# Choosing blocks of expert rows for half of the tokens, and normalising on ScalarE, in a kernel of two post-norm transformer layers

## The reference, cut to what matters

```python
# routing of layer 0; layer 1 is the same with softmax over all experts first, gelu, and hs + 0.3 * moe
logits = xf @ Wr + br                                   # 8 experts
topk_w, topk_idx = jax.lax.top_k(logits, 2)             # 2 chosen per token
gate = sum(one_hot(topk_idx, 8) * softmax(topk_w))
h = relu(einsum('th,ehf->etf', xf, W1) + b1)            # 128 -> 256, every expert
y = einsum('etf,efh->eth', h, W2) + b2                  # 256 -> 128
out = einsum('te,eth->th', gate, y)
layernorm: (x - mean) / sqrt(var + 1e-5)
```

## Time and profile before

| | us |
|---|---|
| median of 3 runs | 1236.21 (1231.8 to 1237.85) |
| the profiled execution's own time | 1233.06 |
| its span, first to last instruction | 1231.1 |
| TensorE busy | 1108.1 |
| VectorE busy | 883.3 |
| ScalarE busy | 753.3 |
| GpSimd busy | 274.9 |
| first expert stage, from its first up to the next attention's first scores | 307.6 to 440.7 |
| second expert stage, to the end | 1100.4 to 1231.1 |

### The profile page before, as it was taken

How to read it: one execution, slowest core, us unless ns; L and a number is a source line. 1 busy time by engine, 2 the same in 40 slices (tenths; PEclk the granted TensorE clock), 3 DMA queues, 4 the chain that set the end, 5 groups by cost and what they waited for, 6 DMA issues and landing times. The chain is left out here.

```text
span 1231.1 us, 24956 instructions
## 1 busy us (share of the span) xinstructions
PE 1108.1 (90%) x8797; PEld 606.1 (49%) x8872; DVE 883.3 (72%) x2136; ACT 753.3 (61%) x1505; POOL 274.9 (22%) x800
## 2 busy tenths in 40 slices
PE   5899998899999989999988998888888878899996
PEld 3466676656777745666555632212112212127775
DVE  3788767783445478888767888988999898914444
ACT  4377656567434426776656667677888767874332
POOL 8134322332002113433333310111101010100000
PEclk9899999999999999999999999999999999999998
DMA  3444343110001600344221311000211100000000
GB/s 87 122 112 110 93 96 89 47 36 8 1 1 27 157 20 31 81 100 101 66 74 31 64 35 30 22 11 15 40 35 34 29 11 17 7 1 1 10 9 18
DMA packets 40058, 57.70 MB, mean 47 GB/s; under 512 B 9495, under 2 KB 15079, under 8 KB 39679
## 3 DMA queue, kind: packets, MB, share of 16 engines
q1 hardware_dynamic: 39934, 56.11, 18.5%
HBM read 30.81 MB, written 24.64 MB: 45 GB/s over the span
## 5 line engine op out<-in xcount | busy, mean ns | idle before, releaser
L838 ACT ACTIVATE probs<-bank 128x512 f32<-128x512 f32 x1088 | 574.7, 603 | 268.9 <-PE bank L1206 267.4
L937 DVE TENSOR_REDUCE tile_max<-bank 128x1 f32<-128x512 f32 (+3 forms) x1152 | 612.0, 593 | 51.4 <-PE bank L1191 47.2
L1191 PE MATMUL bank<-qk 125*128 125x128 bf16 (+2 forms) x1664 | 389.2, 311 | 83.8 <-DVE tile_max L937 65.4
L1206 PE MATMUL bank<-qk 128*128 128x128 bf16 (+4 forms) x1608 | 362.6, 305 | 3.9 <-ACT probs L838 3.6
L1235 PE MATMUL bank<-probs,v_head 128*32 128x512 f32 (+3 forms) x3328 | 304.6, 455 | 0.1
L1191 PEld LDWEIGHTS bank<-qk 125*128 125x128 bf16 (+1 forms) x1664 | 133.6, 97 | 329.1 <-DVE tile_max L937 249.5
L1113 DVE SCALAR_TENSOR_TENSOR acc<-bank,gate,acc 128x128 f32<-128x128 f32 x256 | 72.0, 344 | 143.0 <-PE bank L1364 143.0
L1235 PEld LDWEIGHTS bank<-probs,v_head 128*32 128x32 f32 x3328 | 140.2, 109 | 50.2 <-issue 28.0
L1206 PEld LDWEIGHTS bank<-qk 128*128 128x128 bf16 (+1 forms) x1664 | 134.3, 96 | 52.7 <-ACT probs L838 16.8
L858 ACT ACTIVATE probs<-bank,sb_b 128x512 f32<-128x512 f32 x128 | 80.9, 683 | 123.3 <-PE bank L1353 123.3
L931 DVE TENSOR_REDUCE tile_max<-bank 128x4 f32<-128x512 f32 x128 | 87.4, 688 | 87.5 <-PE bank L1191 87.2
(11 more groups left out here) (130 smaller groups left out, 653.1 us busy)
## 6 DMA issues: line engine op xcount, KB each, us to landing
qk<-qk_parts SPq DMA_DIRECT2D x160, 144.0 KB
qk_parts<-q_parts SPq DMA_DIRECT2D x48, 192.0 KB, 2.4
qk_parts<-k_parts SPq DMA_DIRECT2D x48, 192.0 KB, 3.1
qk_parts<-q_parts SPq DMA_DIRECT2D x24, 96.0 KB, 2.3
qk_parts<-k_parts SPq DMA_DIRECT2D x24, 96.0 KB, 2.9
sb_w<-in_w SPq DMA_DIRECT2D x8, 256.0 KB, 3.8
sb_w<-in_w SPq DMA_DIRECT2D x2, 1024.0 KB, 5.3
qk<-neg_rows SPq DMA_DIRECT2D x96, 6.0 KB
```

The costliest lines, as they stand in the source:

```text
L838: nc.scalar.activation(probs[:, hd.probs_place(c), :], S2[i % len(S2)][:], ACT.Exp, scale=hd.a.scale).then_inc(sem("probs"), 1)
L937: ins = nc.vector.tensor_reduce(tile_max[:, hd.slot, t, which:which + 1], s1[:, at:at + P * count], AX.X, ALU.max)
L1191: ins = mm(s1[:, at:at + P * count], qk[hd.query_rows, hd.place, 0, P * t:P * (t + 1)], qk[hd.query_rows, hd.place, 1, P * k0:P * (k0 + co ...
L1206: ins = mm(s2[:, at:at + P * count], qk[hd.key_rows, hd.place, 1, P * j:P * (j + 1)], qk[hd.key_rows, hd.place, 0, P * q0:P * (q0 + count) ...
```

## The change

**Blocks for sequence 0.** The tokens of sequence 0 no longer go through all experts. Their 2048 pairs of token and chosen expert are laid into blocks of 128 rows of one expert each, `BLOCKS` = 23 (the most that can be needed), in `BLOCK_UNITS` = 6 units of up to 4 blocks. Sequence 1 stays dense: 16 units. So `UNITS` = 22. What this adds:

- Ahead of the stage, in the attention: `ranks` (nine small products that count, for each token and expert, the earlier tokens of that expert), `blocks` (which expert each block belongs to: `expert_i`), `slots` (the row of each pair: `places`), `biases` (`b1` by block), and 16 `scatter` steps, each an indirect DMA from GpSimd that writes 128 tokens' rows to their places in `x_blocks` in DRAM. That buffer is cleared by SyncE after heads 2 and 4 (1.5 MB each, one for each stage). In stage 1 the rows are first transposed back (`mtok`).
- Ahead of up(0), six places `IN_FRONT` without a unit, at which the attention's last steps and the first two `gx` stand. `gx` transposes a unit's rows (loaded from `x_blocks`) on TensorE, and VectorE copies them out.
- For each unit SyncE loads rows and the weights of each block, whose expert it reads from `expert_i` with `value_load`, into the SBUF space of the other stage's weights (two units' worth, used in turn). The load of w1 for unit m+2 waits for up(m), that of w2 for down(m).
- Each unit's result is copied by VectorE to `y_out`, stored by SyncE to `y_blocks`, and after the last one GpSimd gathers 16 x 128 rows by indirect DMA (`gather`, place 19); VectorE adds them with their weights (`combine`, places 26 and 31).
- The gate steps of sequence 0 move from the attention to places 13 to 21 of the stage.

**Normalising on ScalarE.** `normed` is gone. GpSimd computes besides `rstd` also `shift` = -mean * rstd (two more small instructions), and ScalarE does `x = rstd * x_plus + shift`, one instruction a tile. After an attention the two chunks of a sequence are normalised at two places instead of one.

The diff, cut to its core:

```diff
+TOP = 2
+BLOCKS = (TOP * S + E * (P - 1)) // P
+BLOCK_UNITS = -(-BLOCKS // TPC)
+UNITS = BLOCK_UNITS + CB * E
+IN_FRONT = 6
...
+first = at_unit(0, -1, 0)
+put_attention_out(0, 1, first, (0, 1, 2, 3, 4, 5, 6, 7, 9, 10))
+for m, i in enumerate((4, 5, 6, 8, 10, 12)):
+    put(later(first, i), ("gx", 0, m))
...
+            def load_w1(f, m):
+                for j in blocks_of(m):
+                    e = nc.sync.value_load(expert_i[0:1, j:j + 1], min_val=0, max_val=E - 1)
+                    sp.dma_start(block_weights(f)[0][:, TPC * (m % 2) + j % TPC, :],
+                                 inp[f"w1_{f}"][0][:, bass.ds(e, 1), :].rearrange("p a f -> p (a f)")
+                                 ).then_inc(sem(f"w1_in{m % 2}"), 16)
...
+            def first_blocks(f):
+                sp.wait_ge(sem("experts_known"), f + 1)
+                ge(sp, "y_ps", UNITS * f)
+                for m in range(2):
+                    load_w1(f, m)
+                for m in range(2):
+                    load_w2(f, m)
+                sp.wait_ge(sem("scattered"), 16 * TOP * TB * (f + 1))
+                for m in range(2):
+                    load_x(f, m)
+
+            def blocks(f):
+                for m in range(BLOCK_UNITS):
+                    n = len(blocks_of(m))
+                    if m + 2 < BLOCK_UNITS:
+                        taken(sp, "gx", f, m)
+                        load_x(f, m + 2)
+                        sp.wait_ge(sem("hid_ps"), UNITS * f + m + 1)
+                        load_w1(f, m + 2)
+                        sp.wait_ge(sem("y_ps"), UNITS * f + m + 1)
+                        load_w2(f, m + 2)
+                    sp.wait_ge(sem("y_taken"), UNITS * f + m + 1)
+                    sp.dma_start(y_blocks[f].rearrange("(j p) d -> p j d", p=P)[:, TPC * m:TPC * m + n, :],
+                                 y_out[:, m % 2, 0:P * n].rearrange("p (j d) -> p j d", d=D)
+                                 ).then_inc(sem(f"y_stored{m % 2}"), 16)
...
+            def gather(f, c):
+                for m in range(2):
+                    pool.wait_ge(sem(f"y_stored{m}"), 16 * BLOCK_UNITS // 2 * (f + 1))
+                for i in (0, 1):
+                    for t in range(TPC * c, TPC * (c + 1)):
+                        at = TB * i + t
+                        nc.gpsimd.indirect_dma_start(
+                            yg[:, at, :], None, y_blocks[f],
+                            bass.IndirectOffsetOnAxis(ap=places[:, at:at + 1], axis=0)).then_inc(sem(f"gathered{c}"), 16)
...
-            def normed(k, c):
-                dve.wait_ge(sem("rstd"), ROOT_OF[(k, c)])
-                for t in range(TPC * c, TPC * (c + 1)):
-                    ins = nc.vector.tensor_scalar(x[:, t, :], x_plus[:, t, :], mean_var[:, t, 0:1], rstd[:, t:t + 1],
-                                                  ALU.subtract, ALU.mult)
...
+                    if kind == "norm":
+                        k, c = which
+                        act.wait_ge(sem("rstd"), ROOT_OF[(k, c)])
+                        for t in range(TPC * c, TPC * (c + 1)):
+                            ins = nc.scalar.activation(x[:, t, :], x_plus[:, t, :], ACT.Identity,
+                                                       bias=shift[:, t:t + 1], scale=rstd[:, t:t + 1])
```

361 lines of the change are left out of this document (299 added, 62 removed).

## The result

The changed kernel takes **1286.64 us** (median of 4 runs, 1283.25 to 1288.13) against 1234.32 us for the one before in the same measurement: a ratio of 1.042, with a 95% interval of 1.038 to 1.045. It is 52 us slower. The forecast was slower too, but by 15 us: 1251 us. The result lies inside the range of 1220 to 1308.

A forecast was written before the change was run, and what follows sets the result against it. TensorE, busy 90%, was taken as the bound; removed units save 70 us, mostly eaten by SyncE's block loads. Terms 4.3 + 2.5 + 4 + 4 = +14.8 on 1233.1 give 1247.9, stated as 1251 us at the median; range 1220 to 1308.

The forecast's parts named there:

- the pace of the block units: Expert stages, between block units: SyncE's 8 weight loads, one load of rows and one store set a round, 11.7 us.
- rival A: Block rounds: issue is cheap, a load 0.7 us, a round 9.2 us, time 1222 us, faster; chance 0.28.
- The price of a load: SyncE's block weight loads: 0.59 issue, 0.05 gap and 0.65 for reading the expert's number, 1.3 us each.
- First stage: First expert stage: block rounds, dense units and 24 stores make the next attention start at 445.0 instead of 440.7, +4.3 us.
- Second stage: Second expert stage: block rounds and dense units +1.7 us, tail instructions +0.8, together +2.5 us.
- Clock: TensorE at half clock for the first up and its transposes, 2 us in each stage: +4 us, bounds 0 and 20.
- Clears: Attention: two 1.5 MB stores of zeros behind heads 2 and 4 delay heads' maxima, 2 us each: +4 us.
- VectorE's small instructions: Attention: 23 linked instructions, some 7.5 us, set against 7.4 us of normalisings leaving VectorE: zero.
- Scatters: Attention: 16 scatters on GpSimd, two ahead of each splitting of maxima in heads 28 and 29: +1 us.
- Gathers: Dense units: 8 gathers at 1.2 us are done 16 us after the last block unit, before the sums: 0.
- Rival C: Dense units: gathers take 2 us each on GpSimd, sums come late and TensorE waits: +20 us, 1271; chance 0.12.
- B: SyncE's weight loads: reading the number is slow, 1.4 us or more; a load of 2.1 us gives 1325; chance 0.18.

The follow-up runs named there:

- early rows: Changed kernel with SyncE's load of rows for unit m+3 ahead of the wait for down(m): 1299.13 us; with normalising on VectorE and clears in pieces too, 1290.96 us.
- warm16: Changed kernel with 16 idle matmuls on TensorE ahead of the transposes of each block unit from the third on: 1288.52 us, lower level.
- no_software: Changed kernel without the 32 scatters and the 32 gathers, its output lacking the blocks' results: 1285.79 us, ratio 1.042, lower level.
- combo_warm_up: Changed kernel with normalising on VectorE, clears in pieces, rows loaded early, 14 idle matmuls ahead of up's wait for weights: 1259.97 us lower level, 1289.30 us higher.
- clear_spread: Changed kernel with each store of zeros cut into 23 pieces of 64 KB, two behind each of heads 2 to 24: 1303.99 us, one run.

## Why the prediction was right and wrong

Right in sign, and the chance for slower was 0.60; wrong in size, 15 us for 52. The step that failed first is "the pace of the block units": a round was taken as the sum of SyncE's issues, with the landing, the transposes and down hidden behind it, and half the clock within a unit as costing little. The runs showed a closed chain of 13 us through the queue and through TensorE at half clock, where the issues alone are 9.6. Besides it three terms had been put at nothing or near it: normalising on ScalarE (7 us), the end of the third attention (7 us), and half of the clears (4 us). By its own steps, the recorded trace against its marks:

- **What bounds it, what goes.** Right: TensorE's 35 us a stage went, and slower things took their place.
- **The price of a load.** Forecast 1.3 us as 0.59 + 0.05 + 0.65. Measured 1.08, as 0.45 + 0.63. The geometric middle of two far bounds hit the read by luck. The Trainium skill's page "DMA: Bandwidth & Descriptors", section "Latency and other measured facts", puts a tensor_load at about 600 ns at least; the traces agree with 0.63 us, register instructions included. Its section "Issuing engines are not separate DMA queues" calls the sequencer's time to start a DMA usually small; here a round with early rows is SyncE's time, 9.8 us, so this queue is a case where it is not.
- **The pace of the block units.** 11.7 us a round forecast, 12.4 to 13.2 measured, and for another reason: this step failed. By the measured price the issues are only 9.6 us. The rest comes from the order in the queue, where the next rows stand behind the store, and that behind down's weights, which wait for down; and from the clock, below. The nearness of 11.7 is luck: at the forecast's load of 1.3 us rival A's sum for this same chain gives 0.64 + 0.64 + 5.1 + 5.2 = 11.6, so the forecast could not tell the two apart. From the end of up(0) to the end of down(5) the stage took 53.2 us instead of 46.9, in the second 53 to 54. Moving the rows alone gave 18 to 21 us back.
- **First stage.** From the attention's end to up(0) 19.8 us, forecast 19.5. Then +6.3 for the rounds, and +7.9 from down(5) to the last thirds (52.4 for 44.5). Of these 2.8 us are TensorE's waits for normalised tiles and 1.6 one for VectorE:

```profile
PE bank L1566 <- ACT x L963: 2.8, 2, 1.7
PE bank L1597 <- DVE rest L1115: 1.6, 1, 1.6
```

  For the rest I have no row that settles it; 0.8 is a slip of the sum, since its terms 36 + 3.1 + 2 x 3.1 lead from 374.0 to 419.3 and not to 418.5. The 24 stores took 27.8 us for 26.5. Together 137.4 forecast, 153.2 measured.
- **Second stage.** Up(0) 2.0 us later, the rounds 7, the dense units 1.7, the tail 1.5 more than forecast: 14.4 for 2.5.
- **Clock.** Forecast +4, with 20 as the bound if it stays low and the path from rows over down to the next weights gets 2 us longer in each round. That bound describes what happened. The clock stood at 0.82 and 0.71 over the blocks. By the rows of TensorE three rounds of each stage had transposes and down at half clock, 1.6 to 2.2 us more each: an estimated 12 us, nearly all of the 13 by which the rounds miss the forecast. warm16's second stage bears this out, with 11.0 and 11.3 us a round at full clock. The sentence that half the clock costs little while SyncE sets the pace does not apply, because SyncE did not set it. It holds in the version with early rows, where SyncE does.
- **Clears.** +4 forecast, 7.9 measured, twice the size and inside its bounds of 0 to 16. In the other traces with the two large stores it is 8.0 to 11.7.
- **VectorE's small instructions.** Zero forecast, because the normalisings leave the same engine. At the end of the third attention 7.0 us appear. They appear at two places, 3 us between the marks of heads 85 and 86 and 4 between those of 90 and 91, and two runs rule out rivals: it is 7.0 just so in no_software, without scatters and gathers, and in combo_warm_up, with normalising back on VectorE. So the normalisings that leave are worth nothing there, where the sum had set them against the 23. That the 23 instructions make the 7 us, VectorE being full there, stays argued; no run took them out alone.
- **Scatters.** +1 forecast. The first attention's end is 4.6 us late, of which TensorE waits 2.4 us for GpSimd's splittings of maxima, which stand behind scatters (waits between 286 and 320 us: `PE bank L1499 <- POOL neg_parts L855: 2.4, 2, 1.2`). Without scatters (no_software) it is 1.4 us late. The issue price of 1.2 us was right: 0.94 and 0.30 to the next.
- **Gathers.** Zero forecast, right on the recorded level. Rival C's results, late for VectorE, exist on the other level, and its +20 is near the 20 us that the gathers cost there; but this is luck, since GpSimd's pace, which it rested on, is 1.25 us a gather in both.
- **Rivals A and B.** Their prices fell: a load is neither 0.7 us nor over 1.4. But 1.08 is just under the 1.1 that was A's mark, and A's chain is how the rounds are made: with four loads at 1.08 and 2.1 us for the half clock it gives 0.64 + 0.64 + 5.1 + 4.3 + 2.1 = 12.8 us. A itself had 9.2, with loads of 0.7 us and full clock.
- **Normalising on ScalarE**, left out as deciding nothing, costs 7 us in the kernel before: the sum had the length of the passes and not the later start of those who wait for the tile.

So of the span's 55.0 us against the forecast's 14.8, the missing 40 are: the rounds 13 (some 12 of them, by the estimate above, the half clock in the closed chain), the dense units and stores 11 (with a good part of the normalising's 7), the attention stages 16 (clears 4, the end of the first 4.6, the third's end 7, 0.9 elsewhere), the ways into and out of the stages 4, less the 4 that were forecast for the clock.

## What to carry to other kernels

When loads, stores and rows share one queue, write a round as the closed chain through that queue and through the engine that frees the buffers, at the clock that TensorE has after its waits, and only then take the larger of it and the sum of the issues. One transfer moved ahead of a wait gave some 20 us here. A warm clock was worth 2 us a round as long as down stood in the chain, and nothing measurable once it didn't. Ask of each pass moved to another engine when its result is there, not how long it takes. And run the changed kernel itself beside its variants in every set: without that, three variants that gained some 10 to 20 us looked like losses of 13 to 23.

## What the runs showed of the hardware

- The kernel with 64 indirect DMAs of GpSimd has two levels, each holding for a whole set of runs: 1286.6 and 1317 to 1320 us. On the higher one the 32 gathers cost 20 us and the 32 scatters 15, each taken out alone, though an issue takes the same 1.25 us. While the gathers run, instructions of TensorE follow each other at 0.70 us, VectorE takes up results as much as 11 us late, and most completions are missing from the trace (61 of 256 are there). The kernel before, which has none, is at 1233 to 1236 us in every set.
- Reading one number from SBUF into a register of SyncE, with the register instructions that follow, takes 0.63 us a load (1.08 us from load to load with it, 0.45 without).
- Two stores of 1.5 MB, each ahead of a head's small transfers, cost 7.9 us in the recorded trace (5.3 and 2.6); the same bytes in 46 pieces of 64 KB cost nothing that can be seen (clear_spread, 0.6 us ahead at head 12).
- At half clock four 128x128 transposes take 1.11 us instead of 0.60 and a down 3.62 instead of 1.95. This lengthens a round by 2 us where they stand in its chain (13.1 and 13.2 us against 11.3 and 11.0), and by nothing measurable where they don't (1290.96 against 1289.30 us).
- A matmul of 128x128 in fp32 is two records of 0.11 us at full clock: 32 records take 3.74 us (warm16).
